# The delta rule's chunk recurrence run from both ends instead of through transition matrices

## The reference

```python
def delta(x, gates_w, gates_b, lr_w, lr_b, out_w, out_b):
    qkv = x @ gates_w + gates_b
    q, k, v = jnp.split(qkv, 3, axis=-1)
    lr = x @ lr_w + lr_b
    k = k / jnp.linalg.norm(k, axis=-1, keepdims=True)
    K = jnp.tril(jnp.einsum('ntc,nsc->nts', k, k), k=-1)
    A = K + jnp.eye(T)
    u = solve_triangular(A, v, lower=True)
    score = jnp.einsum('nsk,ntk->nst', q, k)      # no causal mask
    y = jnp.einsum('nst,ntv->nsv', score, lr * u)
    return y @ out_w + out_b
```

## Time and profile before

| | us |
|---|---|
| median of 3 runs | 486.85 |
| lowest and highest | 480.68, 499.92 |
| profiled execution | 479.4 |
| its span, first to last instruction | 477.6 |

### The profile page before, as it was taken

How to read it: one execution, slowest core, us unless ns; L and a number is a source line. 1 busy time by engine, 2 the same in 40 slices (tenths; PEclk the granted TensorE clock), 3 DMA queues, 4 the chain that set the end, 5 groups by cost and what they waited for, 6 DMA issues and landing times.

```text
span 477.6 us, 18398 instructions
## 1 busy us (share of the span) xinstructions
PE 404.4 (85%) x7496; PEld 358.9 (75%) x7496; DVE 309.7 (65%) x1555; ACT 259.2 (54%) x654; POOL 174.6 (37%) x196
## 2 busy tenths in 40 slices
PE   2886999889998899988889985999996789889880
PEld 1775898879897799977757864998995477767670
DVE  1577876868768777767763679222035895888564
ACT  3244656556565565646473482346600448886937
POOL 2465433643454534543353557100005684000012
PEclk9997999989999999989999998899999799999986
DMA  6467365556666556656000000000000000000003
GB/s 231 114 144 179 83 155 124 125 147 152 159 159 160 146 134 157 179 130 149 19 2 0 1 0 3 4 4 3 0 1 1 0 2 1 1 3 2 0 2 88
DMA packets 20660, 35.38 MB, mean 74 GB/s; under 512 B 4512, under 2 KB 11680, under 8 KB 20576
## 3 DMA queue, kind: packets, MB, share of 16 engines
q1 hardware_dynamic: 20000, 33.16, 27.8%
q10 hardware_dynamic: 576, 1.05, 0.6%
HBM read 7.85 MB, written 1.05 MB: 19 GB/s over the span
## 4 chain that ended last, share of the span: by engine, by line
PE 60%; DVE 16%; ACT 7%; issue 6%; POOL 4%; SPq 3%; DMA 3%; ACTq 0%; POOLq 0%; DVEq 0%
PE QK L521 9%; PE VY L594 5%; PE O L572 4%; PE S L548 4%; PE PT L558 3%; PE O L663 3%; PE PT L581 3%; SPq L445 2%; PE S L740 2%; PE QK L721 2%; DVE unread_tests L1194 2%; PE S L735 2%; DMA t_swap<-t_sin 2%; POOL qk L1527 2%; PE S L756 2%
## 5 line engine op out<-in xcount | busy, mean ns | idle before, releaser
L1527 POOL TENSOR_TENSOR qk<-t_cos,t_swap 128x512 f32<-128x512 f32 x64 | 80.6, 1280 | 99.9 <-DMA t_swap<-t_sin 97.3
L1285 ACT ACTIVATE probs<-probs,negative_max 128x64 f32<-128x64 f32 x256 | 68.0, 338 | 44.0 <-DVE negative_max L952 43.1
L943 DVE TENSOR_TENSOR t_cos<-QK,cos 128x512 f32<-128x512 f32 x64 | 43.9, 685 | 32.0 <-PE QK L521 16.3
L1566 POOL TENSOR_TENSOR rstd<-var_eps,minus_half 128x4 f32<-128x4 f32 x24 | 25.4, 1057 | 100.3 <-DVE var_eps L996 95.6
L952 DVE CUSTOM_DVE_ANT_0 probs<-S,masks 128x64 f32<-128x64 f32 x256 | 39.4, 219 | 12.8 <-PE S L548 12.7
L943 DVE TENSOR_TENSOR t_sin<-QK,sin 128x512 f32<-128x512 f32 x64 | 43.5, 679 | 0.0
L521 PE MATMUL QK<-xnT,wq 128*128 128x128 f32 x256 | 36.8, 290 | 1.8 <-DVE t_sin L943 1.1
L1306 ACT COPY oT<-PT 128x512 f32<-128x512 f32 x32 | 18.7, 584 | 35.0 <-PE PT L581 34.9
L521 PEld LDWEIGHTS QK<-xnT,wq 128*128 128x128 f32 x256 | 33.6, 205 | 2.8 <-ACT xnT L1316 1.1
L594 PE MATMUL VY<-wo,oT 128*128 128x128 f32 x256 | 34.8, 280 | 0.7 <-ACT oT L1306 0.7
L572 PE MATMUL O<-v_before,probsT 64*32 64x65 f32 x1024 | 29.5, 229 | 7.0 <-issue 7.0
(11 more groups left out here) (277 smaller groups left out, 1100.3 us busy)
## 6 DMA issues: line engine op xcount, KB each, us to landing
t_swap<-t_sin SPq DMA_DIRECT2D x124, 128.0 KB, 2.5
v_before<-v_own SPq DMA_DIRECT2D x32, 132.0 KB
v_before<-v_own SPq DMA_DIRECT2D x62, 66.0 KB
late_tile<-late_weights SPq DMA_DIRECT2D x7, 189.0 KB
x_sb<-x SPq DMA_DIRECT2D x4, 256.0 KB, 4.6
out<-XA SPq DMA_DIRECT2D x4, 256.0 KB, 2.3
cos<-rope_cos SPq DMA_DIRECT2D x3, 256.0 KB, 3.5
sin<-rope_sin SPq DMA_DIRECT2D x3, 256.0 KB, 4.6
```

Of the source, the lines that this page charges most:

```text
L943: last = nc.vector.tensor_tensor(dst[:, u % G, PAIRS * j:PAIRS * j + PAIRS], QK[j][:].rearrange("p (m t) -> p m t", m=PAIRS), table[:, tok ...
L1285: last = nc.scalar.activation(probs[:, u % G, m, e, :], probs[:, u % G, m, e, :], ACT.Exp, scale=-1.0, bias=negative_max[:, u % G, e, m:m ...
L1527: nc.gpsimd.tensor_tensor(qk[:, h, c, WINDOW:WINDOW + P], t_cos[:, h, c], t_swap[:, h, c], ALU.add).then_inc(rope_done, 1)
L1566: nc.gpsimd.tensor_tensor(rstd[:, grp(q)], var_eps[:, grp(q)], minus_half[:, grp(q)], ALU.pow).then_inc(roots_done, 1)
```

## The change

Write the state S of the recurrence as a function of the chunk. G is linear in it, so the first eight chunks can be run forward and the last eight backward: an adjoint matrix R starts from the end and says how G depends on the state that enters a chunk. In the middle one product of R and S closes the sum. Neither side forms transition matrices; each applies its two factors one after the other.

Of a round r, with n = r and last_n = 15 - r: see(r) multiplies the corrected keys of chunk n with S (bank 2) and the keys of chunk last_n with R (bank 4); VectorE subtracts the first from the corrected values in place and the second from the weighted keys in place. update(r) makes keys times values for S (bank 3) and corrected keys times weighted keys for R (bank 5), which VectorE adds to S and R, and two products for G in bank 7. Round 0 has no see. The two chains take turns, in the same order on TensorE and on VectorE. For forward chunks the corrected keys are wanted transposed, so a forward chunk's correction is two matmuls of 128 columns and a backward one's is one of 256. The pairs are corrected from both ends; three before round 0, the other five between see and update and behind update of rounds 0 to 2. The weighted keys get a tile of their own, since keys_T is now read in the rounds; GpSimd's instructions are the same.

```diff
+    MIDDLE = NB // 2
+    PAIR_ORDER = [p for k in range(MIDDLE // 2) for p in (k, NB // 2 - 1 - k)]
...
-        transitions = sb("transitions", [P, NB, 2 * C])
-        state = sb("state", [P, NB, C])
+        state = sb("state", [P, MIDDLE + 1, C])
+        adjoint = sb("adjoint", [P, NB, C])
...
-        weighted_keys = keys_T
+        weighted_keys = sb("weighted_keys", [P, NB, C])
...
                 if t >= 1:
                     right_products(t - 1)
-            for m in range(NB // 2):
-                wait(pe, corrections_kept, m - 1)
-                pe.wait_ge(inverse_kept, TASKS)
+            def correct(k):
+                wait(pe, corrections_kept, k - 1)
                 for i in range(2):
-                    n = 2 * m + i
-                    last = nc.tensor.matmul(B[m % 2][:, 256 * i:256 * i + 256], invT[:, n, :], kv[:, n, 0:2 * C],
-                                            start=True, stop=True)
+                    n = 2 * PAIR_ORDER[k] + i
+                    to = B[k % 2][:, 256 * i:256 * i + 256]
+                    if n < MIDDLE:
+                        nc.tensor.matmul(to[:, 0:C], kv[:, n, 0:C], invT[:, n, :], start=True, stop=True)
+                        last = nc.tensor.matmul(to[:, C:], invT[:, n, :], kv[:, n, C:2 * C], start=True, stop=True)
+                    else:
+                        last = nc.tensor.matmul(to, invT[:, n, :], kv[:, n, 0:2 * C], start=True, stop=True)
                 last.then_inc(corrections_ps, 1)
-            for m in range(NB // 2):
-                pe.wait_ge(corrections_kept, m + 1)
-                pe.wait_ge(weighted_keys_done, m // 2 + 1)
-                wait(pe, transitions_kept, m - 1)
-                for i in range(2):
-                    n = 2 * m + i
-                    nc.tensor.matmul(B[2 + m % 2][:, 256 * i:256 * i + C], corrections[:, n, 0:C], kv[:, n, 0:C],
-                                     start=True, stop=True)
-                    last = nc.tensor.matmul(B[2 + m % 2][:, 256 * i + C:256 * i + 256], corrections[:, n, 0:C], weighted_keys[:, n, :],
-                                            start=True, stop=True)
-                last.then_inc(transitions_ps, 1)
-
-            for n in range(NB):
-                last = nc.tensor.matmul(B[7][:, 0:C], weighted_keys[:, n, :], corrections[:, n, C:], start=(n == 0), stop=False,
-                                        skip_group_check=True)
-                if n < NB - 1:
-                    wait(pe, state_kept, n - 1)
-                    last = nc.tensor.matmul(B[5 + n % 2][:, 0:C], kv[:, n, 0:C], corrections[:, n, C:], start=True, stop=(n == 0),
-                                            skip_group_check=True)
-                if n > 0:
-                    pe.wait_ge(transitions_kept, n // 2 + 1)
-                    pe.wait_ge(state_kept, n)
-                if 0 < n < NB - 1:
-                    last = nc.tensor.matmul(B[5 + n % 2][:, 0:C], transitions[:, n, 0:C], state[:, n, :], start=False, stop=True,
-                                            skip_group_check=True)
-                if n < NB - 1:
-                    last.then_inc(state_ps, 1)
-                if n > 0:
-                    last = nc.tensor.matmul(B[7][:, 0:C], transitions[:, n, C:], state[:, n, :], start=False, stop=(n == NB - 1),
-                                            skip_group_check=True)
-            last.then_inc(g_ps, 1)
+            corrected = lambda n: PAIR_ORDER.index(n // 2) + 1
+            def see(r):
+                n, last_n = r, NB - 1 - r
+                pe.wait_ge(corrections_kept, corrected(n))
+                pe.wait_ge(state_kept, r)
+                nc.tensor.matmul(B[2][:, 0:C], corrections[:, n, 0:C], state[:, r, :], start=True, stop=True).then_inc(values_ps, 1)
+                pe.wait_ge(adjoint_kept, r)
+                nc.tensor.matmul(B[4][:, 0:C], keys_T[:, last_n, :], adjoint[:, last_n + 1, :], start=True,
+                                 stop=True).then_inc(seen_keys_ps, 1)
+            def update(r):
+                n, last_n = r, NB - 1 - r
+                if r > 0:
+                    pe.wait_ge(values_kept, r)
+                else:
+                    pe.wait_ge(corrections_kept, corrected(n))
+                nc.tensor.matmul(B[3][:, 0:C], kv[:, n, 0:C], corrections[:, n, C:], start=True, stop=True).then_inc(state_ps, 1)
+                pe.wait_ge(corrections_kept, corrected(last_n))
+                wait(pe, seen_keys_kept, r)
+                nc.tensor.matmul(B[5][:, 0:C], corrections[:, last_n, 0:C], weighted_keys[:, last_n, :], start=True,
+                                 stop=True).then_inc(adjoint_ps, 1)
+                nc.tensor.matmul(B[7][:, 0:C], weighted_keys[:, n, :], corrections[:, n, C:], start=(r == 0), stop=False,
+                                 skip_group_check=True)
+                nc.tensor.matmul(B[7][:, 0:C], weighted_keys[:, last_n, :], corrections[:, last_n, C:], start=False, stop=False,
+                                 skip_group_check=True)
+            pe.wait_ge(inverse_kept, TASKS)
+            pe.wait_ge(weighted_keys_done, TG)
+            for k in range(3):
+                correct(k)
+            corrections_left = iter(range(3, NB // 2))
+            for r in range(MIDDLE):
+                if r > 0:
+                    see(r)
+                    for k in itertools.islice(corrections_left, 1):
+                        correct(k)
+                update(r)
+                for k in itertools.islice(corrections_left, 1):
+                    correct(k)
+            pe.wait_ge(state_kept, MIDDLE)
+            pe.wait_ge(adjoint_kept, MIDDLE)
+            nc.tensor.matmul(B[7][:, 0:C], adjoint[:, MIDDLE, :], state[:, MIDDLE, :], start=False, stop=True,
+                             skip_group_check=True).then_inc(g_ps, 1)
             pe.wait_ge(g_kept, 1)
             nc.tensor.matmul(B[2][:, 0:C + 1], g_matrix[:], W["w_qT"], start=True, stop=True).then_inc(z_ps, 1)
...
                 else:
                     last = nc.vector.tensor_scalar(rest[SQ:P, grp(q)], packed(2 + t % 2)[SQ:P], -1.0, None, ALU.mult)
                 last.then_inc(rest_kept, 1)
-            for n in range(NB - 1):
-                dve.wait_ge(state_ps, n + 1)
-                if n == 0:
-                    last = nc.vector.tensor_copy(state[:, 1, :], B[5][:, 0:C])
+            for r in range(MIDDLE):
+                n, last_n = r, NB - 1 - r
+                if r > 0:
+                    dve.wait_ge(values_ps, r)
+                    nc.vector.tensor_tensor(corrections[:, n, C:], corrections[:, n, C:], B[2][:, 0:C],
+                                            ALU.subtract).then_inc(values_kept, 1)
+                    dve.wait_ge(seen_keys_ps, r)
+                    nc.vector.tensor_tensor(weighted_keys[:, last_n, :], weighted_keys[:, last_n, :], B[4][:, 0:C],
+                                            ALU.subtract).then_inc(seen_keys_kept, 1)
+                dve.wait_ge(state_ps, r + 1)
+                wait(dve, state_kept, r)
+                if r == 0:
+                    last = nc.vector.tensor_copy(state[:, 1, :], B[3][:, 0:C])
+                elif r < MIDDLE - 1:
+                    last = nc.vector.tensor_tensor(state[:, r + 1, :], state[:, r, :], B[3][:, 0:C], ALU.add)
                 else:
-                    dve.wait_ge(state_kept, n)
-                    last = nc.vector.tensor_tensor(state[:, n + 1, :], state[:, n, :], B[5 + n % 2][:, 0:C], ALU.add)
+                    last = nc.vector.scalar_tensor_tensor(state[:, MIDDLE, :], B[3][:, 0:C], -1.0, state[:, r, :], ALU.mult,
+                                                          ALU.subtract)
                 last.then_inc(state_kept, 1)
+                dve.wait_ge(adjoint_ps, r + 1)
+                wait(dve, adjoint_kept, r)
+                if r == 0:
+                    last = nc.vector.tensor_copy(adjoint[:, last_n, :], B[5][:, 0:C])
+                else:
+                    last = nc.vector.tensor_tensor(adjoint[:, last_n, :], adjoint[:, last_n + 1, :], B[5][:, 0:C], ALU.add)
+                last.then_inc(adjoint_kept, 1)
             dve.wait_ge(g_ps, 1)
             nc.vector.tensor_copy(g_matrix[:], B[7][:, 0:C]).then_inc(g_kept, 1)
             dve.wait_ge(delta_bias_ps, 1)
...
                 else:
                     last = nc.scalar.copy(invT[0:SQ, n, SQ:P], both[0:SQ, :, 1])
                 last.then_inc(inverse_kept, 1)
-            for m in range(NB // 2):
-                act.wait_ge(corrections_ps, m + 1)
-                nc.scalar.copy(corrections[:, 2 * m:2 * m + 2], B[m % 2].rearrange("p (n c) -> p n c", n=2)).then_inc(corrections_kept, 1)
-            for m in range(NB // 2):
-                act.wait_ge(transitions_ps, m + 1)
-                nc.scalar.mul(transitions[:, 2 * m:2 * m + 2], B[2 + m % 2].rearrange("p (n c) -> p n c", n=2), -1.0).then_inc(transitions_kept, 1)
+            for k in range(NB // 2):
```

(12 more changed lines are left out.)

## The result

| us | before | after |
|---|---|---|
| median of 20 executions each | 490.62 | 479.37 |
| lowest and highest | 479.42, 501.15 | 473.44, 493.17 |
| profiled execution | 479.4 | 478.38 |
| its span | 477.6 | 476.6 |
| stretch of the change in it | 29.40 | 20.58 |

The account below looks back on a forecast made before the run. The number of TensorE matmuls was taken to bound the 29.40 us stretch; 2.70 + 8.05 + 10.4 = 21.1 us (or 20.7) saves 8.5, so 486.85 - 8.5 = 478.4 us. Range 471 to 487.

Parts of the forecast that it names:

- (a): The first three correction pairs, ahead of round 0: as before, 2.70 us.
- (b): Rounds 0 to 2, with the five other correction pairs between their matmuls: no stall, 8.05 us.
- (c): Rounds 3 to 7, with no filler but the two g matmuls: period 1.94 us, 1.34 issue and 0.6 stall.
- the walk: Handoff-by-handoff timing of TensorE and VectorE in a late round: second subtract starts after the first ends, period 1.94 us.
- The stretch: From the first correction matmul to the g_matrix copy: 29.40 us before, 21.1 or 20.7 after, saving taken as 8.5.
- the carry: Behind the stretch the same instructions run in the same order, so the 8.5 us saved reach the end.
- rival (5): Clock dips elsewhere move because all that follows comes 8.5 us earlier: some 2 us either way; chance 0.10.
- (2): The clock falls to the 1.2 GHz level in rounds 3 to 7: saving 1.8 us, time 485.1; chance 0.08.
- (3): The clock falls already in round 0 and stays down until the delta matmuls: 10.7 us more, 497.6; chance 0.03.
- (1): In the rounds, answers come back in time for every matmul: saving 9.8 to 11.4 us, time 475.5; chance 0.12.
- (4): The two chains don't overlap in the last five rounds: 9.8 us more, time 488.2, no change; chance 0.07.
- within 2%: Whole kernel: the measured time can't be told from no change, 2% being 9.7 us here; chance 0.56.

Follow-up runs that it names:

- the descent held: The kernel before and the changed kernel, each with four unread bf16 matmuls in every descent step from the fifth on; means 486.7 +- 0.9 and 479.0 +- 0.9 us.
- the shifts: The changed kernel with 10 or 5 more matmuls, giving nothing to the output, behind the last of the stretch; means 483.5 +- 1.5 and 483.6 +- 1.9 us.
- before_warm: The kernel before with bf16 matmuls that nobody reads in TensorE's waits of the MLP and the tail; mean 493.8 +- 2.5 us.
- after_shift5: The changed kernel with 5 more matmuls, giving nothing to the output, behind the last of the stretch; mean 483.6 +- 1.9 us.

## Why the prediction was right and wrong

- Bound by TensorE's matmuls, 28 us of issue to 17.7: right. (a) and (b), no stall in rounds 0 to 2: right. Round 3's A starts 345.89 - 335.11 = 10.78 us into the stretch by the timeline, forecast 2.70 + 8.05 = 10.75.
- (c), rounds 3 to 7: the period is 1.83, not 1.94. The term that was mis-sized is the second subtract, which I let start when the first had ended, 0.33 us behind it; it starts 0.23 behind it. The handoffs themselves hold: 0.05 us from VectorE's end to a load with one wait (348.42 to 348.47) and 0.11 with two (348.65 to 348.76). The Trainium skill, "VectorE: DVE Perf Modes", section "Two Vector instructions with no wait between them", says which Vector instructions are held until every earlier one has finished, by the partitions at which their tiles start. All tiles here start at the first partition, so by that section the second subtract isn't held; the trace agrees (0.23 against 0.29). With 0.23 in place of 0.33 the walk gives 1.84.
- The stretch: 8.8 us saved, forecast 8.5.
- The failed step is: "Behind the stretch the same instructions run in the same order, so I carry 8.5 to the end." The instructions and their order stayed, the granted clock that they met did not, and the sum has no term for it. At equal time at half clock the carry holds (9.4 +- 0.5 us, 8.6 +- 1.1 with the descent held, 7.7 +- 1.3 with it held and nothing else evened out). In the comparison it does not: 9.2 +- 4.0 us more at half clock took 2.8 us back, and in the executions that the ratio goes by 15.0 us more took 4.6 back. The profiled execution lost 7.8 of 8.8: 4.0 behind the stretch, which were the clock, and 3.8 ahead of it, which were not and whose cause is open. I had this as rival (5), with 2 us either way and a chance of 0.10, from one dip of one profile. Measured, the descent alone moves by 0 to 15.6 us (42.4 to 58.0), the tail by 3 and the MLP by 1.
- The base was off as well: the median of three was 486.85, that of twenty 490.62. The forecast time was hit by luck: the base came out 3.8 us higher, and the medians lie 11.25 us apart instead of 8.5, 2.8 more; the two cancel to 1.0. Medians so scattered don't tell 11.25 from 8.5.
- Rivals (2) and (3), the clock falls in the rounds: no. It was 1.00 in each profile of the stretch. (1), no stall: no, 0.49 us in each of five rounds. (4), the chains don't overlap: no.
- Of the chances, within 2% was the likeliest, and it came out so.
- Open: what gives the changed kernel more time at half clock. 0 of 32 executions against 33 of 107 under 44 us are hardly luck, but the shifts could not tell whether its position does it. With the descent held 9 of 12 executions of either kernel are under 44. Open too: what moves the start of the stretch by up to 6 us at nearly equal clock.

## What to carry to other kernels

Where a recurrence splits into two independent halves, running them in turn pays as much as the matmuls it removes, less a stall per round that is the two handoffs minus the issue; work without dependence, dealt out one piece per round and not two in the first rounds, hides that stall. Before a gain of 2% is forecast from one profile, look at how the granted clock differs between executions in the stretches that are not edited: here they spread the executions over 25 us for a gain of 9. To measure such a change, hold the clock where it wavers in both kernels. A comparison at equal time at half clock helps where both kernels have it in the same places; before_warm shows its limit, since taking the half clock out of before's MLP and tail gave nothing, while in the descent each us of it cost 0.3.

## What the runs showed of the hardware

In the descent TensorE's clock can stay at the lower level although the trace shows it busy without a gap: 0.56 over 57.7 us with TensorE busy for 57.1 of them (before_warm, above), 0.54 over 58.0 in after_shift5. Of 233 matmul records from 413 to 464.5 us in before_warm, 89 are single-column or three-column matmuls. Ends of matmuls are modelled, so this busy time is no measure of the work done in it. In other executions of the same instructions it stayed at 1.00 with TensorE busy for 37.8 of 42.4 us. The Trainium skill, "TensorE: Matmul & The Clock Gate", section "What's actually happening", says that the throttled state is the default and activity releases it; taken with the busy time of the trace for activity, a descent like this would have come back to full speed. In these rows it didn't for some 50 us, and the measurement decides: the busy share in a trace doesn't tell whether the clock comes back. With four 128-column bf16 matmuls in each step, the time at half clock in a whole execution was at most 51 us in 30 executions, where before it reached 97 and after 106. Nor did what the Trainium skill says of PSUM bank cycling, weighed in the prediction, show itself: the new rounds, with gaps of 0.2 us and five banks in turn, stayed at 1.00.
